# The experts' products of a decoder layer on one core: matmuls of 512 columns made as two of 256

## The chip, the cores and the metric
One core of a Trainium2 chip runs the whole kernel. The metric is the device time of one execution in microseconds (us), the median of several runs.

## The reference
A pre-norm decoder layer in fp32 on x of shape (8, 256, 512): attention, a convolution over a context, and a mixture of experts, each added to x. Only the last part is touched by the change:

```
probs = softmax(x @ Wr + br); top_vals, top_idx = top_k(probs, 3)      # 12 experts
for e in range(12):
    mask = (top_idx == e).any(-1)
    w_e  = sum of the gate weights of e / max(count of e, 1)
    h    = relu(x @ w1[e] + b1[e])          # 512 -> 1280
    h    = h @ w2[e] + b2[e]                # 1280 -> 512
    out += mask * (w_e * h)
out *= 1 - 0.8 * (sigmoid(relu(mean(out) @ Wp1 + bp1) @ Wp2 + bp2) > 0.7)
```

## The kernel before, in words
The kernel goes through three stages: attention (to about 220 us), the convolution with the router's logits and the routing (to about 540 us), and the experts, in `experts()` from line 1540. Only the last is changed.

Routing sorts the tokens by expert into 59 tiles (NTILE) of 128 rows, each of one expert. For every tile five engines work hand in hand; each runs its own program, written out by hand, and they meet at semaphores:

- POOL gathers the rows of a tile into `xg` and later scatters the result `y` into `acc` in memory.
- PE (TensorE) turns `xg` in four transposes (`x_t`, line 1949, out to `ps_xd`). ACT copies them out as `xf` and rounds them to `xh`; POOL subtracts to get the remainder `xl` (L1808).
- PE makes the **first product** (`first_product`, lines 1955 to 1971): 128 rows by 1280 columns of `h`, in three chunks (CHUNKS: 512, 512 and 256 columns), each in its own bank of `ps_h`. Since values are split into a high and a low part, a chunk is 4 x (xh by w_hi, L1964; xh by w_lo, L1965) and then 4 x (xl by w_hi, L1969): 12 matmuls. xh or xl is the weight that is loaded into the array, the expert's matrix is what streams, so the width of a matmul is the number of columns of the matrix. The matmul that ends a chunk raises `h_done`, and ACT copies the chunk out (L1886) and raises `h_evac`.
- PE turns `h` in ten transposes (`h_t`, L1977), ACT adds the bias and takes the relu (L1895), rounds all of it to `hh` (L1899), and POOL makes the remainder `hl` (L1812).
- PE makes the **second product** (`second_product`, lines 1981 to 1993): 20 matmuls with `hh` (L1987 with w_hi, L1988 with w_lo) and 10 with `hl` (L1991), all 512 columns wide into `ps_y`. The last raises `y_done`, ACT scales `y` out (L1905).

PE's order for tile i is: transposes of h of tile i, first product of tile i+1, transposes of x of tile i+2, second product of tile i. A loop (L2038) holds two tiles; 28 turns of it and three single tiles make the 59. Ahead of each product PE's sequencer reads the number of the expert into a register (`expert_of`, L1943: a TENSOR_LOAD and register operations), since the buffer of the weights (`e % 2`) depends on it. From it come the addresses: ahead of each matmul at L1964, L1965, L1987 and L1988 there is one register operation, ahead of those at L1969 and L1991 none.
DVE meanwhile splits the next expert's weights (L1687, L1689) that SP brings in, and frees a buffer by `h_done` and `y_done` of the first tile of an expert.

## Time and profile before

| | us |
|---|---|
| median of 3 runs | 1478.84 |
| lowest and highest | 1478.68, 1481.39 |
| the profiled execution, its own time | 1480.42 |
| its span, first to last instruction | 1478.6 |

In this span, by the profile's page, PE is busy 1360.2 us, PE's weight loads 1130.1 us (beside the matmuls), DVE 827.3, ACT 697.4, POOL 844.7; the mean granted clock of TensorE is 0.956 of full.

How to read it: PE is the matmuls, PEld the weight loads, PEq or PEldq what PE's sequencer does by itself (reads into registers, register operations, waits). The profile does not count the sequencer's work as busy. A matmul's duration runs over the start of the next one, since they are pipelined: the pace is read from start to start, not from the duration.

### The profile page before, as it was taken

How to read it: one execution, taken by the hardware profiler on the slowest of the kernel's cores; microseconds unless marked ns; L12 is line 12 of the kernel's file. 1: busy time of each engine (PE TensorE's matmuls, PEld its weight loads, DVE VectorE, ACT ScalarE, POOL GpSimd, SP SyncE). 2: the span in 40 equal slices, each digit the busy share in tenths (PEclk: the TensorE clock that was granted, in tenths of full speed). 3: DMA queues.
4: the chain of work that ended last, by engine and by line, in shares of the span. 5: the costliest groups of instructions: out<-in, count | busy, mean ns of one | idle time of the engine just before them, and what ended most of it. 6: DMA issues, size and time to landing. Idle time of an engine off the chain costs nothing.

```text
span 1478.6 us, 27777 instructions
## 1 busy us (share of the span) xinstructions
PE 1360.2 (92%) x7868; PEld 1130.1 (76%) x7869; DVE 827.3 (56%) x1197; ACT 697.4 (47%) x1878; POOL 844.7 (57%) x955
## 2 busy tenths in 40 slices
PE   5899998799996369999999999999999999999993
PEld 4677776577775258888888888888888888888883
DVE  6788887499997986647174435547443553000013
ACT  3656666154553424445444454544445444444530
POOL 0456545244564056767677677676766767565540
PEclk8999999799997679999999999999999999999996
DMA  7000000163333425545264435446443543251146
GB/s 271 1 1 0 0 0 27 47 214 100 105 112 114 185 77 159 125 116 157 47 169 102 121 87 133 107 109 170 106 126 81 139 106 78 37 162 35 29 133 237
DMA packets 77576, 152.42 MB, mean 103 GB/s; under 512 B 9120, under 2 KB 13728, under 8 KB 77024
## 3 DMA queue, kind: packets, MB, share of 16 engines
q1 hardware_dynamic: 62496, 115.09, 24.6%
q0 software_dynamic: 14320, 35.40, 12.1%
q10 hardware_dynamic: 720, 1.44, 0.3%
q8 instruction: 21, 0.34, 0.1%
q14 instruction: 19, 0.16, 0.0%
HBM read 119.31 MB, written 32.59 MB: 103 GB/s over the span
## 4 chain that ended last, share of the span: by engine, by line
PE 61%; DMA 2%; SPq 0%; DVE 0%; issue 0%; ACT 0%; DVEq 0%; POOL 0%; POOLq 0%
PE ps_h L1964 9%; PE ps_h L1965 9%; PE ps_h L1969 9%; PE ps_y L1987 9%; PE ps_y L1988 9%; PE ps_y L1991 9%; PE ps_td L1977 4%; PE ps_xd L1949 2%; DMA w_lo<-acc 1%; DMA w_hi<-acc 1%; DMA xg<-xnd,gi 0%; DMA acc<-y,si 0%; PE ps_xd L1998 0%; SPq L1673 0%; SPq L1668 0%
## 5 line engine op out<-in xcount | busy, mean ns | idle before, releaser
L1964 PE MATMUL ps_h<-w_hi,xh 128*128 x708 | 247.0, 361 | 1.5 <-ACT xh L1880 1.4
L1965 PE MATMUL ps_h<-w_lo,xh 128*128 x708 | 242.2, 354 | 0.0
L1987 PE MATMUL ps_y<-w_hi,hh 128*128 x590 | 236.9, 402 | 0.0
L1988 PE MATMUL ps_y<-w_lo,hh 128*128 x590 | 231.9, 393 | 0.0
L1689 DVE TENSOR_TENSOR w_lo<-stage,w_hi 128x512 f32 x220 | 214.4, 975 | 28.6 <-DVE w_hi L1687 2.9
L1822 POOL TENSOR_TENSOR y<-y,b_sb 128x512 f32<-128x512 f32 x58 | 80.1, 1382 | 210.2 <-ACT y L1905 210.2
L1812 POOL TENSOR_TENSOR hl<-h,hh 128x1280 fp32r<-128x1280 f32 x59 | 182.9, 3100 | 16.7 <-ACT hh L1899 16.2
L1886 ACT ACTIVATE h<-ps_h 128x512 f32<-128x512 f32 x177 | 80.6, 527 | 198.6 <-POOL hl L1812 190.9
L1905 ACT ACTIVATE y<-ps_y,wt 128x512 f32<-128x512 f32 x59 | 40.6, 688 | 275.4 <-PE ps_y L1991 275.4
L1969 PE MATMUL ps_h<-w_hi,xl 128*128 x708 | 164.1, 354 | 0.0
L1895 ACT ACTIVATE h<-ps_td,b_now 128x128 f32<-128x128 f32 x590 | 158.6, 391 | 3.9 <-PE ps_td L1977 1.2
L1964 PEld LDWEIGHTS ps_h<-w_hi,xh 128*128 128x128 f32 x708 | 133.6, 189 | 22.3 <-issue 2.2
L1965 PEld LDWEIGHTS ps_h<-w_lo,xh 128*128 128x128 f32 x708 | 133.6, 189 | 20.3
L1687 DVE CAST w_hi<-stage 128x512 f32 x220 | 143.8, 654 | 6.5 <-DMA stage<-in_wcat 6.0
L1991 PE MATMUL ps_y<-w_hi,hl 128*128 x590 | 144.9, 392 | 0.0
L1730 DVE TENSOR_TENSOR turn<-cst 128x1 f32<-128x1 f32 x11 | 3.7, 333 | 241.0 <-PE ps_h L1969 241.0
L1969 PEld LDWEIGHTS ps_h<-w_hi,xl 128*128 128x128 f32 x708 | 119.8, 188 | 19.0
L1991 PEld LDWEIGHTS ps_y<-w_hi,hl 128*128 128x128 f32 x590 | 110.8, 188 | 24.4
L1988 PEld LDWEIGHTS ps_y<-w_lo,hh 128*128 128x128 f32 x590 | 111.5, 189 | 22.5
L1987 PEld LDWEIGHTS ps_y<-w_hi,hh 128*128 128x128 f32 x590 | 111.5, 189 | 22.1
L1837 POOL DMA_INDIRECT acc<-y,si x59 | 101.4, 1719 | 27.2 <-issue 14.8
L1808 POOL TENSOR_TENSOR xl<-xf,xh 128x512 fp32r<-128x512 f32 x59 | 78.0, 1321 | 38.5 <-ACT xh L1880 37.8
(256 smaller groups left out, 2566.7 us busy)
## 6 DMA issues: line engine op xcount, KB each, us to landing
stage<-in_wcat SPq DMA_DIRECT2D x220, 256.0 KB
front<-in_ctx_rev SPq DMA_DIRECT2D x32, 192.0 KB, 2.4
w_lo<-in_wcat SPq DMA_DIRECT2D x4, 1280.0 KB, 12.2
acc<-added_c POOLq DMA_DIRECT2D x1, 4352.0 KB, 17.4
front<-kpad SPq DMA_DIRECT2D x16, 256.0 KB, 3.4
toe<-kpad SPq DMA_DIRECT2D x16, 256.0 KB, 3.4
x2d<-xs SPq DMA_DIRECT2D x16, 256.0 KB, 2.4
xnd<-xn_c SPq DMA_DIRECT2D x16, 256.0 KB, 2.0
```

What stands on the lines that cost most here:

```text
L1687: nc.vector.tensor_copy(hi, stage[:, c % NSTAGE]).then_inc(w_rounded, 1)
L1689: nc.vector.tensor_tensor(lo, stage[:, c % NSTAGE], hi.bitcast(F32), ALU.subtract).then_inc(split_done, 1)
L1812: nc.gpsimd.tensor_tensor(hl[:], h[:], hh[:].bitcast(F32), ALU.subtract).then_inc(hl_ready, 1)
L1837: pool.indirect_dma_start(acc, bass.IndirectOffsetOnAxis(ap=si[:, par:par + 1], axis=0), y[:, par], None, compute_op=ALU.add).then_inc(add ...
L1886: nc.scalar.activation(h[:, lo:hi], ps_h[:, c, 0:hi - lo], ACT.Copy).then_inc(h_evac, 1)
L1895: last = nc.scalar.activation(h[:, k * P:(k + 1) * P], ps_t[:, k // 4, (k % 4) * P:(k % 4 + 1) * P], ACT.Relu, bias=b1_now[:, k:k + 1])
L1964: nc.tensor.matmul(out, x_hi, part(w_hi, e, k * FF + lo, hi - lo), start=(k == 0), stop=False)
L1965: nc.tensor.matmul(out, x_hi, part(w_lo, e, k * FF + lo, hi - lo), start=False, stop=False)
L1969: last = nc.tensor.matmul(out, xl[:, k * P:(k + 1) * P], part(w_hi, e, k * FF + lo, hi - lo), start=False, stop=(k == KD - 1))
L1987: nc.tensor.matmul(ps_y[:], h_hi, part(w_hi, e, KD * FF + k * D, D), start=(k == 0), stop=False)
L1988: nc.tensor.matmul(ps_y[:], h_hi, part(w_lo, e, KD * FF + k * D, D), start=False, stop=False)
L1991: last = nc.tensor.matmul(ps_y[:], hl[:, k * P:(k + 1) * P], part(w_hi, e, KD * FF + k * D, D), start=False, stop=(k == KF - 1))
```

## The change
Both products are made in pieces of 256 columns (HALF_N). In the first product each chunk of 512 is done as two halves in sequence: all 12 matmuls of the left half, then all 12 of the right, into the two halves of the same bank; `h_done` is still raised once, behind the second half. The second product is done as two halves of 30 matmuls, `y_done` once behind the second. The wait for `xl_ready` and that for `hl_ready` stand in the first half alone, so they come after 8 and 20 matmuls of 256 columns.

```diff
--- before.py
+++ after.py
@@ -1576,6 +1576,7 @@
         ps_x = psum("ps_xd", [P, 512])
         ps_h = psum("ps_h", [P, 3, 512])
         ps_y = psum("ps_y", [P, 512])
+        HALF_N = 256
         CHUNKS = [(0, 512), (512, 1024), (1024, FF)]
         ps_pool, ps_late = ps_x[:, 0:KD * B], [ps_h[:, 1 + n, 0:KD * B] for n in range(LATE)]
         ps_hid, ps_z = ps_t[:, 0], ps_t[:, 1, 0:B]
@@ -1956,18 +1957,19 @@
                 pe.wait_ge(split_done, e * NCHUNK + N1)
                 pe.wait_ge(xh_ready, i + 2)
                 for c, (lo, hi) in enumerate(CHUNKS):
-                    out = ps_h[:, c, 0:hi - lo]
                     if not first:
                         pe.wait_ge(h_evac, 3 * i + c - 2)
-                    for k in range(KD):
-                        x_hi = xh[:, k * P:(k + 1) * P]
-                        nc.tensor.matmul(out, x_hi, part(w_hi, e, k * FF + lo, hi - lo), start=(k == 0), stop=False)
-                        nc.tensor.matmul(out, x_hi, part(w_lo, e, k * FF + lo, hi - lo), start=False, stop=False)
-                    if c == 0:
-                        pe.wait_ge(xl_ready, i + 2)
-                    for k in range(KD):
-                        last = nc.tensor.matmul(out, xl[:, k * P:(k + 1) * P], part(w_hi, e, k * FF + lo, hi - lo),
-                                                start=False, stop=(k == KD - 1))
+                    for at in range(lo, hi, HALF_N):
+                        out = ps_h[:, c, at - lo:at - lo + HALF_N]
+                        for k in range(KD):
+                            x_hi = xh[:, k * P:(k + 1) * P]
+                            nc.tensor.matmul(out, x_hi, part(w_hi, e, k * FF + at, HALF_N), start=(k == 0), stop=False)
+                            nc.tensor.matmul(out, x_hi, part(w_lo, e, k * FF + at, HALF_N), start=False, stop=False)
+                        if at == 0:
+                            pe.wait_ge(xl_ready, i + 2)
+                        for k in range(KD):
+                            last = nc.tensor.matmul(out, xl[:, k * P:(k + 1) * P], part(w_hi, e, k * FF + at, HALF_N),
+                                                    start=False, stop=(k == KD - 1))
                     last.then_inc(h_done, 1)
 
             def h_t(i):
@@ -1982,14 +1984,18 @@
                 pe.wait_ge(split_done, e * NCHUNK + NCHUNK)
                 pe.wait_ge(hh_ready, i + 1)
                 pe.wait_ge(y_evac, i + 1)
-                for k in range(KF):
-                    h_hi = hh[:, k * P:(k + 1) * P]
-                    nc.tensor.matmul(ps_y[:], h_hi, part(w_hi, e, KD * FF + k * D, D), start=(k == 0), stop=False)
-                    nc.tensor.matmul(ps_y[:], h_hi, part(w_lo, e, KD * FF + k * D, D), start=False, stop=False)
-                pe.wait_ge(hl_ready, i + 2)
-                for k in range(KF):
-                    last = nc.tensor.matmul(ps_y[:], hl[:, k * P:(k + 1) * P], part(w_hi, e, KD * FF + k * D, D),
-                                            start=False, stop=(k == KF - 1))
+                for at in range(0, D, HALF_N):
+                    out = ps_y[:, at:at + HALF_N]
+                    for k in range(KF):
+                        h_hi = hh[:, k * P:(k + 1) * P]
+                        nc.tensor.matmul(out, h_hi, part(w_hi, e, KD * FF + k * D + at, HALF_N), start=(k == 0), stop=False)
+                        nc.tensor.matmul(out, h_hi, part(w_lo, e, KD * FF + k * D + at, HALF_N), start=False, stop=False)
+                    if at == 0:
+                        pe.wait_ge(hl_ready, i + 2)
+                    for k in range(KF):
+                        last = nc.tensor.matmul(out, hl[:, k * P:(k + 1) * P],
+                                                part(w_hi, e, KD * FF + k * D + at, HALF_N),
+                                                start=False, stop=(k == KF - 1))
                 last.then_inc(y_done, 1)
 
             def pool_early(b):
```

On PE's queue, in the loop, at the end of the part with `xh` of the first chunk of the first product (`ps_h` is the chunk's bank, `w_hi` and `w_lo` the matrix; an ISA row is a register operation of two steps, a REGISTER_ALU row one of one step; the loads of the weights xh and xl aren't listed, there is one ahead of each matmul). Before:

```order
L1964 MATMUL ps_h<-w_hi,xh 128x512
L1965 REGISTER_ALU
L1965 MATMUL ps_h<-w_lo,xh 128x512
L1969 MATMUL ps_h<-w_hi,xl 128x512 [waits xl_ready]
L1969 MATMUL ps_h<-w_hi,xl 128x512 x3
L1961 REGISTER_ALU
L1964 ISA [waits h_evac]
L1964 MATMUL ps_h<-w_hi,xh 128x512
```

and with the change:

```order
L1966 MATMUL ps_h<-w_hi,xh 128x256
L1967 REGISTER_ALU
L1967 MATMUL ps_h<-w_lo,xh 128x256
L1971 MATMUL ps_h<-w_hi,xl 128x256 [waits xl_ready]
L1971 MATMUL ps_h<-w_hi,xl 128x256 x3
L1966 ISA
L1966 MATMUL ps_h<-w_hi,xh 128x256
L1967 REGISTER_ALU
```

Behind the four matmuls with xl there now stands the right half of the same chunk, with its own register operations and without a wait; before, the next chunk stood there.

The same engine at the end of the part with `hh` of the second product, before:

```order
L1987 MATMUL ps_y<-w_hi,hh 128x512
L1988 REGISTER_ALU
L1988 MATMUL ps_y<-w_lo,hh 128x512
L1989 REGISTER_ALU
L1991 MATMUL ps_y<-w_hi,hl 128x512 [waits hl_ready]
L1991 MATMUL ps_y<-w_hi,hl 128x512 x9
L1974 REGISTER_ALU
L1977 MATMUL ps_td<-cst,h 128x128 [waits relu_done,h_evac]
```

and with the change:

```order
L1991 MATMUL ps_y<-w_hi,hh 128x256
L1992 REGISTER_ALU
L1992 MATMUL ps_y<-w_lo,hh 128x256
L1994 REGISTER_ALU
L1996 MATMUL ps_y<-w_hi,hl 128x256 [waits hl_ready]
L1996 MATMUL ps_y<-w_hi,hl 128x256 x9
L1991 ISA
L1991 MATMUL ps_y<-w_hi,hh 128x256
```

The matmuls with hl, and the wait for it, come after the first 20 of 256 columns; the right half follows, and only then the transposes of the next tile. In a tile the matmuls go from 66 to 120 beside the 14 transposes, those with a register operation ahead from 44 to 80; the loop's body goes from 440 to 728 instructions of PE (matmuls, weight loads, register operations).

## Rows read from the trace of the kernel before
**Rows 1.** The page: busy time by engine, slices of PE, granted clock.
```profile
PE 1360.2 (92%) x7868; PEld 1130.1 (76%) x7869; DVE 827.3 (56%) x1197; ACT 697.4 (47%) x1878; POOL 844.7 (57%) x955
...
PE   5899998799996369999999999999999999999993
...
PEclk8999999799997679999999999999999999999996
```
**Rows 2.** Busy time in the stretch 560 to 1400 us, all engines.
```profile
core 0: us, PE busy (x) PEld busy (x) DVE busy (x) ACT busy (x) POOL busy (x), PEclk, DMA share, GB/s
560.00:1400.00 840.00, 840.00 (x4397) 713.69 (x4396) 346.04 (x453) 395.73 (x989) 574.84 (x659) 1.00 0.43 109
```
**Rows 3.** The waits from 560 to 1397 us, the four largest.
```profile
engine line waited for: us in total, times, longest us
ACT y L1905 <- PE ps_y L1991: 243.7, 54, 4.8
DVE turn L1730 <- PE ps_h L1969: 241.0, 10, 35.5
POOL y L1822 <- ACT y L1905: 195.0, 55, 4.1
ACT h L1886 <- POOL hl L1812: 181.5, 55, 3.8
```
**Rows 4.** The chain of waits from 890 to 960 us: start, us, what.
```profile
892.71 2.29 PE ps_y L1991 x10
895.00 1.09 PE ps_td L1977 x10
...
900.68 0.92 PE ps_h L1969 x4
902.51 0.46 PE ps_h L1969 x4
...
953.85 2.29 PE ps_y L1991 x10
```
**Rows 5.** Timeline of PE in three tiles: start, us from start to end, instruction.
```profile
901.44 0.28 PE L1964 MATMUL ps_h<-w_hi,xh 128*128 x1
...
902.35 0.62 PE L1969 MATMUL ps_h<-w_hi,xl 128*128 x4
902.80 0.60 PE L1949 MATMUL ps_xd<-cst,xg 128*128 128x128 f32 x4
903.16 0.48 PE L1987 MATMUL ps_y<-w_hi,hh 128*128 x1
903.48 0.40 PE L1988 MATMUL ps_y<-w_lo,hh 128*128 x1
...
907.83 2.46 PE L1991 MATMUL ps_y<-w_hi,hl 128*128 x10
910.12 1.25 PE L1977 MATMUL ps_td<-cst,h 128*128 128x128 f32 x10
...
932.01 0.28 PE L1964 MATMUL ps_h<-w_hi,xh 128*128 x1
...
932.92 0.62 PE L1969 MATMUL ps_h<-w_hi,xl 128*128 x4
933.38 0.60 PE L1949 MATMUL ps_xd<-cst,xg 128*128 128x128 f32 x4
...
953.69 2.46 PE L1991 MATMUL ps_y<-w_hi,hl 128*128 x10
```
**Rows 6.** PE's queue, L1987 and L1988, 947 to 950.3: ns, first and last start.
```profile
L1987 PEldq FUSED_REGOPS  x10: 46/46/118, 947.8 to 950.1; - x10
L1988 PEldq ALU_OP  x10: 32/32/32, 948.0 to 950.2; - x10
```
**Rows 7.** PE's queue by line: L1965, L1961 near 910; L1982, L1984 near 947.
```profile
L1965 PEldq ALU_OP  x4: 32/32/32, 909.5 to 910.3; - x4
L1961 PEldq ALU_OP  x1: 32/32/32, 910.6 to 910.6; - x1
L1982 PEldq FUSED_REGOPS  x1: 47/47/47, 947.6 to 947.6; - x1
L1984 PEldq EVENT_SEMAPHORE  x1: 51/51/51, 947.7 to 947.7; - x1
```
**Rows 8.** PE's queue at the first read of the expert, L1943 and L1964.
```profile
L1943 PEldq FUSED_REGOPS  x2: 42/96/151, 954.2 to 954.6; - x2
L1943 PEldq TENSOR_LOAD <-eid x1: 306/306/306, 954.3 to 954.3; - x1
L1964 PEldq FUSED_REGOPS  x6: 46/46/104, 955.2 to 956.8; - x6
```
**Rows 9.** PE's queue at the second read, L1943, in four tiles; L1987 after one.
```profile
L1943 PEldq FUSED_REGOPS  x2: 42/96/151, 946.9 to 947.3; - x2
L1943 PEldq TENSOR_LOAD <-eid x1: 299/299/299, 947.0 to 947.0; - x1
L1943 PEldq TENSOR_LOAD <-eid x1: 1002/1002/1002, 763.5 to 763.5; - x1
L1943 PEldq TENSOR_LOAD <-eid x1: 1019/1019/1019, 1222.1 to 1222.1; - x1
L1943 PEldq FUSED_REGOPS  x2: 42/96/151, 824.6 to 825.8; - x2
L1943 PEldq TENSOR_LOAD <-eid x1: 1056/1056/1056, 824.7 to 824.7; - x1
L1987 PEldq FUSED_REGOPS  x1: 118/118/118, 826.3 to 826.3; - x1
```
**Rows 10.** Timeline of ACT and POOL and of PE near 947; hl in all tiles.
```profile
945.06 1.27 ACT L1899 ACTIVATE hh<-h 128x1280 fp32r<-128x1280 f32 x1
946.42 3.21 POOL L1812 TENSOR_TENSOR hl<-h,hh 128x1280 fp32r<-128x1280 f32 x1
949.02 0.48 PE L1987 MATMUL ps_y<-w_hi,hh 128*128 x1
L1812 POOL TENSOR_TENSOR hl<-h,hh x55: 2945/3014/3539, 564.0 to 1389.4; 128x1280 fp32r<-128x1280 f32 x55
```
**Rows 11.** DMA queue that loads code, 600 to 1390 us: packets, MB, share of 16 engines.
```profile
q14 instruction: 1, 0.01, 0.0%
```

## The prediction
> **What bounds the kernel now.** I read the page's busy line and slices first [rows 1]: TensorE (PE) is busy 92% of the span and from the sixteenth slice on nearly without a gap, at the full granted clock. That stretch is the experts' loop. Then the busy time of one stretch of it [rows 2]: from 560 to 1400 us PE is busy 840.00 of 840.00 us at a clock of 1.00, its weight loads (PEld) 713.69 us. In the waits of the same stretch [rows 3] everybody waits for PE or for POOL, and no row has PE as the one that waits. So here a nanosecond of PE's pace is a nanosecond of the kernel, and all else counts only if it comes to stop PE. The chain of waits [rows 4] gives the period: from one run of ten L1991 to that four tiles later 953.85 - 892.71 = 61.14 us, 15.285 us for a tile, 59 tiles.
>
> **Term 1: the pace of the matmuls.** Per tile the change turns 24 matmuls of 512 columns in the first product and 30 in the second into 108 of 256; 12 of 256 and 14 transposes stay. The columns streamed are the same; the weight loads of these go from 54 to 108. What a matmul of 256 costs when it stands in a row of its like is to be seen already, in the third chunk. In start times [rows 5]: the ten L1991 take 910.12 - 907.83 = 2.29 us, and the 19 matmuls ahead of them 907.83 - 903.48 = 4.35 us, so 0.2289 us at 512 columns. The twelve of the third chunk take 902.80 - 901.44 = 1.36 us, in another tile 933.38 - 932.01 = 1.37 us, and their first eight 0.91 us in both. That is 0.1136 us each with the turn to the transposes in it, and between 0.905/8 = 0.1131 and 0.915/8 = 0.1144 without. The weight loads do not stop it: the transposes, one load for each 128 columns, go at 1.09/10 = 0.109 us [rows 4], below 0.1133. I take 0.1134: two halves are 0.2268 us against 0.2289, 2.1 ns less. 54 x 59 = 3186 pairs x 2.1 ns = 6.7 us gained. The ends: 2.7 ns, 8.6 us gained, and 0.1 ns, 0.3 us gained.
>
> The Trainium skill ("TensorE: Matmul & The Clock Gate", section "Back-to-back issue gap") has a matmul cost its columns at 2.4 GHz and about 2.5 ns on top, so that two of 256 would cost 2.5 ns more than one of 512; by it this term would be 3186 x 2.5 ns = 8.0 us lost. The rows at 0.1133 and 0.2289 do not show such a fixed part; they show a price a little under proportion.
>
> **Term 2: whether PE's sequencer can feed it.** This is new. Each matmul and each weight load has to be issued, and ahead of each matmul with xh or hh stands one register instruction that works out an address. In the rows of PE's queue [rows 6] the ten L1987 register operations go from 947.8 to 950.1 and the ten L1988 ones from 948.0 to 950.2: 2.2/9 = 0.244 us for two matmuls, 0.122 each. That is slower than the array at 256 columns (0.1134), where at 512 it had twice the time. A matmul without one (L1969, L1991) costs the sequencer far less. Bounds: from the last L1965 at 910.3 to L1961 at 910.6 [rows 7] it issues one matmul that belongs to the register operation and four more, 0.3 - 0.1 = 0.2 us, 0.05 each, though the queue was full there, so this is a ceiling. And register operations with nothing between them (L1982 at 947.6, L1987 at 947.8, one between) stand 0.1 apart, with a matmul between them 0.122: 0.02 each is the floor. I take 0.03, nearer the floor because the ceiling has waiting in it.
>
> A piece of 12 (8 with a register operation, 4 without) then costs the sequencer 8 x 0.122 + 4 x 0.03 = 1.10 us and the array 12 x 0.1134 = 1.36. A half of the second product: 20 x 0.122 + 10 x 0.03 = 2.74 against 3.40. So on average it keeps up. The trouble can only be where it stands still: it reads the expert's number twice a tile (L1943). How far it is ahead there: the first read begins at 954.2 [rows 8], when the array has started three of the ten L1991 that began at 953.69; the other seven and the ten transposes are queued, **17 matmuls**. Before the change that is 7 x 0.229 + 10 x 0.109 = 2.7 us of cover, after it 7 x 0.1134 + 1.09 = 1.88. Its next register operation of the product is at 955.2, so with the first issue some 1.2 us go by: 0.7 us of lead is left. Five pieces of 12 win 0.26 us each, three waits cost 0.1 each: +1.0, so the queue is nearly full again at the second read. There the cover is 13 x 0.1134 + 0.44 = 1.91 us; a read of 0.30 us costs 1.05 us (946.9 to 947.8 and the issue), one of 1.056 us, the longest [rows 9], 1.8 us (824.6 to 826.3 and the issue). Then the 20 matmuls with register operations lose 20 x 0.009 = 0.17 us more. So only reads over some 0.8 us run the array dry, for about 0.2 us each. There are six of them over 0.9 us in the 59 tiles (three stand in the rows); with one a little shorter that is 7 x 0.2 = **1.4 us lost**. The two ends: nothing, and the first rival.
>
> **Terms at nothing.** The second product's first half reaches the hl matmuls after 20 x 0.1134 = 2.27 us instead of 4.58, and hl comes from POOL. In the tile shown [rows 10] POOL ends hl at 946.42 + 3.21 = 949.63; the second product starts at 949.02, so hl is asked for at 951.3 and is 1.7 us early. The longest hl takes 3.54 us instead, 0.3 us later; 1.3 us stay. With that cover gone PE would wait for each hl by the shortfall. hh, which the sequencer waits for at L1984, ends at 945.06 + 1.27 = 946.33, 1.4 us before it gets there (947.7). xl for a tile is made in the tile before. h_done and y_done still come once a chunk and once a tile, so ACT, DVE and SP see the same events. The loop's code grows from 440 to 728 PE instructions; from 600 to 1390 us the trace has a single load of code [rows 11], so the loop of 440 stayed in place, and no row shows a loop of 728.
>
> **Sum.** -6.7 + 1.4 = -5.3 us. The profiled execution took 1480.4 us for a span of 1478.6, 1.6 us over the median of 1478.84 of the three runs. Against its own time that is 1475.1; against the median, **1473.5 us**. What a measurement of this kernel can tell from no change is about 0.2%, 3 us: 1475.9 to 1481.8.
>
> **Rivals.**
> First, the slower side: **the sequencer becomes the bound.** If a matmul without register operation costs it 0.05 us (the ceiling) and not 0.03, its work for a tile is 80 x 0.122 + 54 x 0.05 + 1.2 for the first read, 1.3 for the second with its longer ones and 0.5 for waits and the loop's branch = 15.5 us, against the array's 15.285 - 0.11 = 15.17. Then the lead is never won back and each tile takes some 15.4 to 15.5: 59 x (15.45 - 15.285) = +9.7, about 1488 us. It decides at about 0.045 us a matmul, or with 0.03 at about 0.13 us for one with a register operation. For it: 0.122 is already over 0.1134, and the margin is 5% of a tile. Against it: the ceiling was read where the queue was full.
> The Trainium skill ("TensorE: Matmul & The Clock Gate", section "Architectural detail: the array is 16× 32×32, not 1× 128×128") gives TensorE a queue of 64 instructions; that would be 32 matmuls with their loads, where [rows 5, 8] show 17, and with it term 2 would be nothing and the time 1472.1.
>
> Second: **two halves cost what the whole did.** The chain [rows 4] has the four L1969 of 256 at 0.46 us and of 512 at 0.92: no gain. Then term 2 alone is left: 1478.84 + 1.4 = 1480.2. If that 0.46/4 = 0.115 is the pace of long stretches and 0.2289 stays that of the wide ones, a fixed part of each matmul shows, two halves lose 1.1 ns, and 3.5 us more give 1483.7. The fixed part that the Trainium skill states (page and section as under term 1) would be larger than this. For it: three stretches of 12 are all that a trace of before shows, and rounded. Against it: 0.91 us for eight, twice.
>
> Third: **hl late.** It would need hl 1.3 us later than its longest; then 1 us a tile would be 59 us, a time of 1532. POOL's work does not change, so I give it next to nothing.
>
> **How the numbers follow.** The forecast has 0.64 (1470.2 to 1475.9, from 8.6 gained and nothing lost to a gain of 3); the second rival 0.19, most of it within 0.2%; the first 0.15 and the third 0.02. Faster 0.64; same 0.18; slower 0.18. The range leaves out the first rival's upper half and the third: 1470.2 to 1485.
>
> **What would show it.** In the profile of after: PE busy all of 560 to 1390 us or with idle time of a few us in all, on L1991's successor (the first matmuls with hh) right after the second read; a tile of 15.17 to 15.2 us; twelve matmuls in 1.36 us in every chunk, thirty in 3.40 in each half of the second product; no wait of PE for hl or hh. Wrong would be: twelve in more than 1.38 us (the second rival), pitches of 0.122 us through whole stretches with register operations (the first), a wait of PE for hl L1812, or loads of code in every turn of the loop.

## The result and the profile after

| | us |
|---|---|
| changed kernel, median of 4 runs | 1502.46 (1501.01 to 1503.20) |
| kernel before, median of 4 runs on the same chip | 1478.76 (1475.79 to 1481.39) |
| ratio, 95% interval | 1.016 (1.0139 to 1.0181) |
| profiled execution, its own time and span | 1501.01, 1499.2 |

The change costs 23.7 us; the forecast was 5 us gained. Five more runs of it in a later comparison gave 1499.51 to 1501.58. The ratios and intervals given below count only runs within 1.5% of the fastest run of the same kernel.

The page of the changed kernel, busy time, to hold against [rows 1]:

```profile
PE 1382.3 (92%) x11054; PEld 1288.8 (86%) x11055; DVE 823.3 (55%) x1197; ACT 697.3 (47%) x1878; POOL 834.2 (56%) x955
```

PE is busy 22.1 us longer, and the span is longer by nearly the same (20.6); POOL is busy 10 us less, DVE and ACT 4 us or less away from before. The same stretch as in [rows 2]:

```profile
560.00:1400.00 840.00, 840.00 (x7184) 840.00 (x7183) 337.64 (x448) 384.95 (x960) 551.57 (x644) 1.00 0.44 107
```

PE is again busy all of 840.00 us at a granted clock of 1.00, so no gap and no slower clock took the time. What is new is that the weight loads fill the stretch as well, 840.00 us against 713.69. The waits of 560 to 1397 us, as in [rows 3], have the same partners as before; the two longest, shown here, have grown by some 15 us each. Still none is PE's:

```profile
ACT y L1906 <- PE ps_y L1996: 260.3, 53, 5.2
DVE turn L1731 <- PE ps_h L1971: 255.7, 10, 37.9
```

So PE works without a break, and each step takes longer. The chain of waits (start, us, what), against [rows 4]:

```profile
899.19 1.18 PE ps_y L1996 x10
900.37 1.09 PE ps_td L1979 x10
...
902.41 0.47 PE ps_h L1971 x4
...
908.54 0.44 PE ps_xd L1950 x4
...
930.54 1.18 PE ps_y L1996 x10
```

From 899.19 to 930.54 are two tiles: 15.675 us each against 15.285 before. 0.39 x 59 = 23.0 us, the whole loss within 1 us. Ten matmuls of 256 columns take 1.18 us; the transposes are unchanged at 1.09 and 0.44. The timeline of PE (start, us from start to end, instruction) over three pieces of twelve and the third chunk:

```profile
902.72 0.28 PE L1966 MATMUL ps_h<-w_hi,xh 128*128 x1
...
906.96 0.28 PE L1966 MATMUL ps_h<-w_hi,xh 128*128 x1
...
908.37 0.60 PE L1950 MATMUL ps_xd<-cst,xg 128*128 128x128 f32 x4
```

Three pieces from 902.72 to 906.96 are 36 matmuls in 4.24 us: **0.1177 us each**, not 0.1134. The last piece, 906.96 to 908.37, is the third chunk, whose instructions the change did not touch: 1.41 us for twelve, where [rows 5] have 1.36 and 1.37. Whatever it is, it sits in the pace of every 256-wide matmul, old or new.

The sum closes with it. Two halves cost 0.2354 us for 0.2289: 6.5 ns x 3186 pairs = 20.7 us. The third chunk: 12 x 4.4 ns x 59 = 3.1 us. Together 23.8 us, measured 23.7.

Does the sequencer cause it? Its register operations are the L1991 and L1992 rows, the read is L1944 (queue rows near 908 of the changed kernel: count, ns min/median/max, first and last start):

```profile
L1944 PEldq TENSOR_LOAD <-eid x1: 939/939/939, 906.7 to 906.7; - x1
L1991 PEldq FUSED_REGOPS  x20: 46/46/113, 908.2 to 913.0; - x20
L1991 PE MATMUL ps_y<-w_hi,hh x13: 279/279/365, 908.7 to 912.8; 128*128 x13
```

Even behind a read of 939 ns the first register operation stands half a microsecond ahead of its matmul. And the four matmuls with xl, which have no register operation, go at 0.47/4 = 0.1177 like the rest. Matching every register operation with its matmul between 600 and 1390 us gives the same for the whole stretch: they stand 3 to 18 matmuls ahead of the one that the array has started. So the array goes slower while its queue has work for it.

The trace of before had shown the same in its first two tiles, and the prediction did not look at them. The chain of the kernel before from 541 to 567 us:

```profile
541.75 0.47 PE ps_h L1969 x4
...
550.89 0.47 PE ps_h L1969 x4
...
566.20 0.46 PE ps_h L1969 x4
```

In its timeline the twelve of the third chunk go from 549.79 to 551.20 (1.41 us) in one tile and from 565.13 to 566.50 (1.37 us) in the next. So a 256-wide matmul with its load has **two paces here: 0.1133 and 0.1177 us**. Of the 59 third chunks in the trace of before the first two are slow and the other 57 quick; the changed kernel runs at the slow pace. The experiments ask what holds it there.

### The profile page after: what moved, and what is told of

It is laid out like the page before. It is cut to its first block, busy times and chain, and to the rows that moved or that the text cites. A ratio compares the mean times of both kernels' runs of the same rounds, so it can differ in the third digit from the quotient of the medians.

```text
span 1499.2 us, 36273 instructions
## 1 busy us (share of the span) xinstructions
PE 1382.3 (92%) x11054; PEld 1288.8 (86%) x11055; DVE 823.3 (55%) x1197; ACT 697.3 (47%) x1878; POOL 834.2 (56%) x955
## 3 DMA queue, kind: packets, MB, share of 16 engines
q0 software_dynamic: 14320, 35.40, 12.3%
## 4 chain that ended last, share of the span: by engine, by line
PE 61%; DMA 2%; POOL 0%; SPq 0%; issue 0%; ACT 0%; DVE 0%; DVEq 0%; POOLq 0%
PE ps_h L1971 9%; PE ps_h L1966 9%; PE ps_h L1967 9%; PE ps_y L1996 9%; PE ps_y L1991 9%; PE ps_y L1992 9%; PE ps_td L1979 4%; PE ps_xd L1950 2%; DMA w_hi<-acc 1%; DMA w_lo<-acc 1%; DMA xg<-xnd,gi 0%; DMA acc<-y,si 0%; SPq L1674 0%; POOL hl L1813 0%; POOL acc L1838 0%
## 5 line engine op out<-in xcount | busy, mean ns | idle before, releaser
L1966 PE MATMUL ps_h<-w_hi,xh 128*128 x1180 | 296.6, 284 | 1.5 <-ACT xh L1881 1.4
L1967 PE MATMUL ps_h<-w_lo,xh 128*128 x1180 | 291.5, 280 | 0.0
L1991 PE MATMUL ps_y<-w_hi,hh 128*128 x1180 | 289.5, 284 | 0.0
L1992 PE MATMUL ps_y<-w_lo,hh 128*128 x1180 | 284.5, 280 | 0.0
L1966 PEld LDWEIGHTS ps_h<-w_hi,xh 128*128 128x128 f32 x1180 | 222.0, 188 | 2.1 <-issue 2.1
L1992 PEld LDWEIGHTS ps_y<-w_lo,hh 128*128 128x128 f32 x1180 | 222.7, 189 | 0.0
L1991 PEld LDWEIGHTS ps_y<-w_hi,hh 128*128 128x128 f32 x1180 | 222.7, 189 | 0.0
L1967 PEld LDWEIGHTS ps_h<-w_lo,xh 128*128 128x128 f32 x1180 | 222.4, 188 | 0.0
L1971 PEld LDWEIGHTS ps_h<-w_hi,xl 128*128 128x128 f32 x1180 | 160.0, 188 | 0.3 <-POOL xl L1809 0.3
L1996 PEld LDWEIGHTS ps_y<-w_hi,hl 128*128 128x128 f32 x1180 | 147.1, 188 | 0.3 <-POOL hl L1813 0.3
```

What stands on the lines that cost most here:

```text
L1966: nc.tensor.matmul(out, x_hi, part(w_hi, e, k * FF + at, HALF_N), start=(k == 0), stop=False)
L1967: nc.tensor.matmul(out, x_hi, part(w_lo, e, k * FF + at, HALF_N), start=False, stop=False)
L1971: last = nc.tensor.matmul(out, xl[:, k * P:(k + 1) * P], part(w_hi, e, k * FF + at, HALF_N), start=False, stop=(k == KD - 1))
L1991: nc.tensor.matmul(out, h_hi, part(w_hi, e, KD * FF + k * D + at, HALF_N), start=(k == 0), stop=False)
L1992: nc.tensor.matmul(out, h_hi, part(w_lo, e, KD * FF + k * D + at, HALF_N), start=False, stop=False)
L1996: last = nc.tensor.matmul(out, hl[:, k * P:(k + 1) * P], part(w_hi, e, KD * FF + k * D + at, HALF_N), start=False, stop=(k == KF - 1))
```

## The experiments

In what follows "quick" is 0.1133 us and "slow" 0.1177 us for a matmul of 256. By the sizes above a kernel's time is worked out as: each pair of halves -2.1 ns quick or +6.5 ns slow, x 59, and 3.1 us more if the third chunk is slow. Diffs are against the changed kernel unless said otherwise; 59 is the number of tiles. Experiments 1, 2, 3, 7, 8, 9 and 12 are a single execution each.

**1. Who stands ahead: the narrow chunk first.** The kernel before, with only the order of widths changed, so that the chunk of 256 comes right behind the ten transposes of h.

```diff
-        CHUNKS = [(0, 512), (512, 1024), (1024, FF)]
+        CHUNKS = [(0, 256), (256, 768), (768, FF)]
```

> The kernel before, with the chunk of 256 columns first and the two of 512 behind it, so that the same twelve matmuls of 256 now come right behind the ten transposes of h instead of behind a matmul of 512. Theory A (a run of 256 keeps the pace that it gets at its start: 0.1133 us behind a 512, 0.1177 behind a transpose): twelve in about 1.41 us instead of 1.36, the tile 0.05 us longer, about 1482 us in all. Theory B (0.1177 comes from the weight loads having no rest anywhere in the tile): 0.1133 us as before, twelve in 1.36, 1478.8 us. Theory C (the sequencer's issue): 0.1133 as before, since twelve matmuls are covered by its lead, 1478.8 us.

One run: 1482.52 us, the nine runs of before beside it 1476.44 to 1481.24 (median 1478.98). In its chain:

```profile
895.51 1.09 PE ps_td L1977 x10
897.54 0.47 PE ps_h L1969 x4
899.85 0.91 PE ps_h L1969 x4
```

The narrow chunk is slow in every tile, the chunks of 512 unchanged: 3.1 us expected from the pace, 3.5 measured. The chain shows it; the time alone would not, since the runs of before spread over 4.8 us. The same twelve matmuls, moved from behind 512-wide ones to behind transposes, are slow. Neither their number nor the register operations changed.

**2. Only the second chunk in halves.** Second product and first chunk stay whole (`wide = HALF_N if c == 1 else hi - lo`).

> Only the second chunk of the first product is made in halves: 36 matmuls of 256 in a row behind twelve of 512; the rest as before. Theory A: all 36 at 0.1133 us, 4.08 us in all, the tile 0.027 us shorter, about 1477 us. Theory B: the pace is between the two or falls from 0.1133 to 0.1177 within the run, up to 4.24 us for the 36 and 1486 us. Theory C: the matmuls behind a register operation drift towards 0.122 us once the lead is used, those with xl stay at 0.1133.

One run: 1478.24 us, where 12 pairs x 2.1 ns x 59 = 1.5 us less than before were to be had, below what one run can tell. 36 matmuls of 256 stand in a row behind twelve of 512, quick in all tiles but the first. Its chain:

```profile
897.37 0.45 PE ps_h L1972 x4
```

**3. Only the second product in halves.** The first product as before.

> Only the second product is made in halves; the first as before. Theory A: the 60 behind the transposes of x go at 0.1177 us, 7.06 us instead of 6.87; the chunk of 256 in the first product stays at 0.1133 (1.36 us for twelve); about +0.19 us a tile, 1490 us. Theory B: the 60 between 0.1133 and 0.1177, and the chunk of 256 slower too. Theory C: as A in the part with hh, but the matmuls with hl at 0.1133.

One run: 1474.81 us, quick in all tiles but the first and the end of the last, though the 60 stand right behind the four transposes of x. Theory A as it stood, that any transposes ahead make the pace slow, is false. Its chain:

```profile
902.61 1.13 PE ps_y L1995 x10
...
917.81 1.14 PE ps_y L1995 x10
```

**4. A 512-wide matmul at the head of each product** of the changed kernel:

```diff
+                nc.tensor.matmul(ps_y[:], hh[:, 0:P], part(w_hi, e, KD * FF, D), start=True, stop=False)
                 for at in range(0, D, HALF_N):
...
+                        if k:
+                            nc.tensor.matmul(out, h_hi, part(w_hi, e, KD * FF + k * D + at, HALF_N), start=False, stop=False)
```

> The changed kernel, but the first matmul of each product (k = 0 with the high part of the matrix) is 512 wide over both halves, so that every run of 256 begins behind a 512. Theory A: all 256-wide matmuls at 0.1133 us, a tile of about 15.17 us, 1472 us: faster than both. Theory B and C: no change against the changed kernel, 0.1177 us, a tile of 15.67 us, 1502 us.

Five runs, 1503.87 us (1501.21 to 1505.05), ratio 1.0166 (1.0151 to 1.018). Slow everywhere. One wide matmul at the entry does not do it.

**5. The first tiles wide.** The first four tiles stand outside the loop with matmuls of 512; only the last second product ahead of the loop, and everything in it, is in halves. It asks whether the start decides.

```diff
-            with pe.Fori(0, PAIRS) as j:
+            for j in range(WIDE_PAIRS):
+                tile(2 * j, j, 0, True, True, True)
+                tile(2 * j + 1, j, 1, True, True, True)
+            with pe.Fori(WIDE_PAIRS, PAIRS) as j:
```

> The changed kernel, but the first four tiles of the experts' stage are taken out of the loop and made as before the change (first products of 512, 512 and 256 columns, second products of 512, the last of them in halves); the loop of the other 26 pairs is all in halves. Theory D (a 256-wide run has two paces, 0.1133 and 0.1177 us; the state is carried through transposes and kept by 256-wide runs, and only stretches of 512 switch it): the second product before the loop is at 0.1133 and so is every tile of the loop, 15.17 us a tile, about 1472 us. Theory E (the quick pace needs a stretch of 512 in every tile): 0.1177 us from the first product of the loop on, 15.67 us a tile, about 1501 us.

Four runs, 1500.05 us (1499.45 to 1501.51), ratio 1.0136 (1.0117 to 1.0154). Its chain shows the quick pace being lost:

```profile
601.94 1.14 PE ps_y L1999 x10
603.08 1.09 PE ps_td L1981 x10
605.11 0.47 PE ps_h L1973 x4
```

The second half of the second product is quick (1.14), the ten transposes follow, and from the next matmul of 256 on the loop is slow to its end. A quick start is not enough.

**6. First chunk wide**, the rest in halves (`wide = hi - lo if c == 0 else HALF_N`), so that twelve matmuls of 512 stand between the transposes of h and the first of 256.

> The changed kernel, but the first chunk of the first product is 512 wide: behind the ten transposes of h stand twelve matmuls of 512, and all the rest of the tile is 256 wide. Theories D and E both allow the quick pace: 96 and 12 matmuls of 256 at 0.1133 us, a tile of 15.19 us, 1473 us, if twelve of 512 are enough; if they are not, 0.1177 us and about 1498 us.

Four runs, 1497.33 us (1496.26 to 1499.63), ratio 1.0123 (1.0102 to 1.0144). Quick at first, until this second product, in its timeline:

```profile
627.07 0.28 PE L1992 MATMUL ps_y<-w_hi,hh 128*128 x1
...
628.20 0.28 PE L1992 MATMUL ps_y<-w_hi,hh 128*128 x1
...
628.65 0.28 PE L1992 MATMUL ps_y<-w_hi,hh 128*128 x1
...
629.01 0.28 PE L1993 MATMUL ps_y<-w_lo,hh 128*128 x1
```

Ten steps from 627.07 to 628.20 are 0.113 each; from 628.65 on they are 0.12, and stay at 0.1177 for the rest of the loop. Just ahead of this the sequencer had read the expert's number, and its register operations (queue rows, L1944 and, from 628.5 to 629.0 us, L1993):

```profile
L1944 PEldq TENSOR_LOAD <-eid x1: 1034/1034/1034, 624.8 to 624.8; - x1
L1993 PE MATMUL ps_y<-w_lo,hh x3: 276/278/280, 628.3 to 628.8; 128*128 x3
L1993 PEldq ALU_OP  x2: 32/32/32, 628.6 to 628.8; - x2
```

Here the register operations (628.6, 628.8) have the matmuls of the same line (at 628.77 and 629.01 in the timeline) only some 0.2 us behind them, with the weight load in between: the array, at 0.113 a matmul, had used up its queue behind a read of 1.03 us and met the sequencer at its 0.122. The place coincides; that it is the cause, this run alone does not show. Until then five tiles in a row had been quick, with all but the first chunk in halves.

**7. Second chunk wide**, the first in halves right behind the ten transposes.

> As the run before, but the second chunk is the wide one and the first is in halves: the 24 behind the transposes of h are 256 wide, then twelve of 512, then 256 for the rest. If what counts is what stands behind the transposes of h (as when the narrow chunk was put first), the 24 go at 0.1177 us and those behind the wide chunk may go at either: 0.1133 us if twelve of 512 switch the state, a tile of 15.30 us and 1480 us; 0.1177 us if not, 1499 us.

One run: 1498.5 us, slow throughout. 42 pairs x 6.5 ns x 59 + 3.1 = 19.2 us over the 1478.8 of before give 1498.0.

**8. One transpose of h more** (the first is made twice, eleven in a row), to shift the phase by 0.109 us.

> The changed kernel with the first of the ten transposes of h made twice (0.109 us more a tile, 6.4 us in all). If the pace hangs on the instant at which the run of 256 begins behind the transposes, one more may switch it: 0.1133 us and 1478 us. If it does not hang on that (theory E, and D in its plain form), 0.1177 us stays and the time is 1509 us.

One run: 1507.94 us; slow in the whole loop, and 0.109 x 59 = 6.4 us for the transpose. An odd number did no better than an even one. The second product of the last tile, behind the 48 small matmuls of the pooling, begins at the half clock. When the clock is back it is quick, in a kernel whose products have no matmul of 512 (a window with its granted clock of 0.50, and the chain):

```profile
1466.40:1469.40 3.00, 3.00 (x15) 3.00 (x15) 0.00 (x0) 0.00 (x0) 3.00 (x3) 0.50 0.61 87
...
1470.20 1.13 PE ps_y L1996 x10
```

**9. Twelve transposes of h** in the kernel of experiment 5.

> The kernel with the wide prologue (e6), in which the pace of 0.1133 us held through the four transposes of x and was lost behind the ten of h, with two of the ten transposes of h made twice, so twelve (0.218 us more a tile, 12.9 us in all). If what decides is the instant at which the run of 256 begins, and four transposes keep the pace, so do three times four: 0.1133 us in the loop until the array catches up with the sequencer somewhere, 1485 us if it never does. If ten or more transposes always lose it: 0.1177 us from the first product of the loop on, 1513 us.

One run: 1514.49 us. The second product ahead of the loop was slow already, so this run can't say what the number does. Its trace shows two things beside that. Four third chunks ahead of the loop, all behind 24 matmuls of 512, alternate: slow, quick, slow, quick (0.47, 0.46, 0.47 and 0.46 us for the four with xl at 549.44, 564.96, 580.50 and 596.02). And the slow second product comes straight behind the last, quick one: the pace was lost across the four transposes of x.

**10. The read moved.** Experiment 6, with the expert's number for the second product read behind the first chunk, where the queue holds 512-wide matmuls.

```diff
                     last.then_inc(h_done, 1)
+                    if then is not None and c == 0:
+                        read = then()
```

> The kernel with the first chunk wide and all else in halves (e7), but the read of the expert's number for the second product is issued right behind the first chunk of the first product instead of ahead of the second product, where the sequencer has most lead. Theory F (the state of 256-wide runs falls from 0.1133 to 0.1177 us when the array catches up with the sequencer, as it did in e7 at 628.7 us behind a long read, and then stays there though the queue is full again): the array never catches up, 0.1133 us in all tiles, a tile of 15.19 us, about 1473 us, faster than before. Theory G (the fall in e7 had nothing to do with the sequencer): as e7, some 1497 us, with a fall early in the stage.

Fourteen runs in two heaps: six from 1470.17 to 1475.87 us and eight from 1496.26 to 1501.28, nothing between. The sizes give 42 pairs x 2.1 ns x 59 = 5.2 us gained in the quick case, 1472.7 against the 1477.86 of before in this comparison, and 19.2 lost in the slow one, 1497.1. The middles of the heaps are 1472.8 and 1497.9. The ratio, 0.9964 (0.9949 to 0.998), is that of the first heap alone; as a kernel it is a coin toss. The profiled run was one of the upper heap, and its first product in the loop was still quick; the second product behind it, four transposes of x later, was slow, and all of the loop from there on:

```profile
547.04 0.46 PE ps_h L1972 x4
...
550.29 1.18 PE ps_y L2000 x10
```

The register operations of that second product begin at 546.31 us for a matmul at 547.89, 15 matmuls ahead, so here the pace was lost with a well filled queue. That moving the read brought the lower heap isn't shown either: with eight of fourteen in the upper one, experiment 6 would have all of its four there by chance in one case of nine.

**11. The second product alone, timed.** The kernel of experiment 3 once more.

> The kernel of e2 once more, timed in rounds: only the second product in halves. 0.1133 us for its 60 matmuls in all tiles but the first, 30 x 2.1 to 2.3 ns = 0.063 to 0.069 us a tile less than before, 3.7 to 4.1 us in all: about 1475 us, ratio 0.997.

Twelve runs: nine from 1471.45 to 1477.28 us (middle 1473.46) and three of 1491.22, 1493.09 and 1493.67. The ratio 0.9989 (0.9964 to 1.0015) counts eleven of them, those of 1491.22 and 1493.09 us too; the middle of the nine is 0.997 of before's 1477.86. Worked out: 1474.1 quick, 1492.5 slow. The profiled run was one of the three, and its chain stands beside that of experiment 3, for **the same code**:

```profile
894.12 1.18 PE ps_y L1995 x10
...
902.84 0.47 PE ps_h L1970 x4
...
909.65 1.18 PE ps_y L1995 x10
```

A tile takes 909.65 - 894.12 = 15.53 us here and 15.20 us in experiment 3. From 600 to 1400 us the two traces agree in what else is seen: a granted clock of 1.00, weight loads busy 748 and 747 of 800 us, a DMA share of 0.43 in both. So the pace isn't a property of the instructions; it is a state that an execution gets into and keeps. Here too it was lost across the four transposes of x, in the first second product of the loop, and the 24 matmuls of 512 in every tile behind it did not bring it back once.

**12. The second read made twice**, in the kernel of experiment 3, to let the array catch up with the sequencer in every tile.

> The kernel with only the second product in halves (e2, 0.1133 us in all tiles), with the read ahead of the second product made twice, some 0.5 us more in which the sequencer issues nothing. Theory F: the array catches up in the second product, which falls to 0.1177 us or more in many tiles, up to 0.26 us a tile beside the delay itself; 1485 to 1495 us; the 24 matmuls of 512 may bring the pace back each time. Theory G: only the delay, at most 0.1 to 0.2 us where reads are long, the pace stays 0.1133; about 1478 us.

One run: 1498.82 us. Its chain from 560 to 600 us:

```profile
564.44 0.46 PE ps_h L1970 x4
...
567.95 1.18 PE ps_y L1995 x10
...
580.22 0.47 PE ps_h L1970 x4
...
595.73 0.46 PE ps_h L1970 x4
```

The third chunk, behind 24 matmuls of 512, finds the quick pace in two of these three tiles, and the second products behind the doubled read are slow by their end here. From 547 us on nine of 58 third chunks are quick, the last at 1141 us. So a stretch of 512 can bring the quick pace back but need not.

The doubled read lets the array catch up: the register operations then stand two matmuls ahead and now and then a matmul starts late. In such a place the pace changes, and in both directions. At 598.2 and at 865.0 us a quick second product turns slow. At 1098 us a slow one turns quick (timeline, then chain):

```profile
1097.09 0.28 PE L1991 MATMUL ps_y<-w_lo,hh 128*128 x1
...
1097.68 0.33 PE L1990 MATMUL ps_y<-w_hi,hh 128*128 x1
...
1099.34 1.13 PE ps_y L1995 x10
```

Five steps to 1097.68 take 0.59 us, 0.118 each; then come matmuls that start late, and the ten with hl take 1.13 us. It stayed quick until the queue ran low again in the next tile. No matmul of 512 stands in between. The time is some 6 us over what experiment 11 took at the slow pace; the second read may have cost them, and they were not taken apart.

**13. The first product alone in halves**, right behind the ten transposes; the second product whole.

> Only the first product in pieces of 256; the second stays in matmuls of 512. The pieces of 256 stand right behind the ten transposes of h. Theory A (256-wide matmuls keep one of two paces, 0.1133 or 0.1177 us, for as long as they follow each other; behind the ten transposes of h they always take the slow one): all 60 at 0.1177 in every tile, 24 pairs x 6.5 ns + 12 x 4.4 ns = 0.209 us a tile, x 59 = 12 us more, about 1490 us, in every one of the timed runs. Theory B (the pace of the expert stage is drawn once per execution, and the place does not matter): some runs near 1475 us with 0.1133 everywhere, some near 1490.

Six runs, 1491.32 us (1488.91 to 1492.92), before 1478.02, ratio 1.0091 (1.0075 to 1.0107). Slow in every run, by its time, as Theory A has it: 12.3 us worked out, 13.3 measured. In its chain the narrow matmuls are slow and the ten of 512 with hl take what they took before:

```profile
895.74 2.29 PE ps_y L1993 x10
...
900.07 0.47 PE ps_h L1971 x4
```

It also splits the change: about 12 us of its loss come with the first product, which includes the third chunk's 3.1, and 30 pairs x 6.5 ns x 59 = 11.5 us with the second.

**14. Ten transposes of x.** Experiment 3's kernel with six more transposes of x: each of the four a second time and two a third.

```diff
-                for k in range(KD):
+                for k in (*range(KD), *range(KD), KD - 2, KD - 1):
                     last = nc.tensor.transpose(ps_x[:, k * P:(k + 1) * P], xg[:, par, k * P:(k + 1) * P], ident)
```

> The kernel with the second product alone in halves, and x turned with ten transposes for four (six are made twice): is it the number of transposes ahead of the 256-wide matmuls that loses the fast pace? The six more cost 6 x 0.109 us x 59 = 38.6 us. Theory A (number of transposes ahead decides): always slow behind them, 30 pairs x 6.5 ns + 12 x 4.4 ns = 0.248 us a tile, 14.6 us more than the fast runs of the same kernel without the six, so 1473 + 38.6 + 14.6 = about 1526 us every time. Theory B (it is something else than their number, such as what stands ahead of the transposes: here 512-wide and 256-wide matmuls of the first product): mostly 1512 us, some runs at 1526, as without them.

Six runs, 1530.19 us (1527.92 to 1537.13). All slow by their times, where with four transposes nine of twelve were quick. In the chain, 1.09 for the ten, then 1.18:

```profile
891.46 1.09 PE ps_xd L1950 x10
894.91 1.18 PE ps_y L1995 x10
```

It agrees with Theory A, number and all (1526 expected). But the third chunk behind the 512-wide ones is slow too (907.15, 0.47 for four), as in the trace of experiment 11, so here both places share the pace; in those of experiments 9 and 12 they did not always.

**15. The changed kernel again.**

> The changed kernel once more, timed more often. Theory A (both products behind or fed by the slow stretch behind the transposes of h): every run between 1500 and 1505 us. Theory B (drawn per execution, as with the second product alone in halves, where a quarter of the runs were slow): some runs near 1476 us (1478.8 less the 6.7 us of the forecast's first term, and with the code and reads as they are).

Five runs, 1500.27 us (1499.51 to 1501.58), before 1478.02, ratio 1.0154 (1.0138 to 1.0171). By their times none of the nine runs was quick. Yet the profiled one was, for a while. Its chain, the four matmuls with xl of three pieces of twelve; the ten transposes of h stand between the first and the second:

```profile
537.57 0.47 PE ps_h L1971 x4
...
541.16 0.59 PE ps_h L1971 x4
...
542.65 0.45 PE ps_h L1971 x4
```

Behind the transposes the matmuls were slow at first (540.41 to 540.88 in the timeline, four in 0.47 us). The sequencer was then only two matmuls ahead, two matmuls started 0.02 and 0.10 us late, and from 541.25 on the pace was quick, within a row of matmuls of 256. It held through the rest of the first product, the four transposes of x and the second product:

```profile
553.30 1.14 PE ps_y L1996 x10
556.47 0.47 PE ps_h L1971 x4
```

The same step as in experiment 5: quick ahead of the ten transposes, slow behind them, and slow for the rest of the loop.

**16. No long row of transposes.** If that row is the cause, breaking it up must help. The transposes of h of the next tile go in pairs between the last ten matmuls with hl:

```diff
+                        if at and then_t and k % 2:
...
+                            h_part((k - 1, k))
```

> The changed kernel, with the ten transposes of h of the next tile no longer in a row: two of them behind every second one of the last ten matmuls with hl, the last two behind the last. So never more than four 128-wide transposes follow each other. Theory A (a long row of transposes right ahead of the 256-wide matmuls loses the fast pace of 0.1133 us): fast in many or all of the runs, 1478 - 6.7 = 1471 us, and 4 more turns from transposes to matmuls a tile at some 8 ns (28 + 201 against 113 + 109 ns) give 2 us back: about 1473. Theory B (256-wide matmuls of this kernel run at 0.1177 whatever stands between them): every run at 1501 to 1505 us.

Five runs, 1503.55 us (1502.88 to 1505.71), ratio 1.0181 (1.0165 to 1.0196). Slow in every run, by its time; a piece in its timeline:

```profile
920.76 0.63 PE L1971 MATMUL ps_h<-w_hi,xl 128*128 x4
922.17 0.63 PE L1971 MATMUL ps_h<-w_hi,xl 128*128 x4
```

1.41 us from one piece of twelve to the next. Theory A falls: in a loop of 256-wide matmuls alone a long row of transposes is not needed to stay at the slow pace. (This trace had it from the stage's first tiles on, so it does not show what a pair of transposes does to a quick pace.)

**17. Its control:** the kernel before with the same placing in pairs.

> The control: the kernel before, all chunks and the second product as there (512 wide), with the same placing of the transposes in pairs between the last ten matmuls with hl. Theory A: the pace of the 512-wide matmuls is the same with either history (0.2289 us), so placing alone brings nothing: 1476 to 1481 us. Theory B: the same. Should the placing itself be worth something (relu and hh of the next tile start no earlier), it shows here.

Twelve runs, 1480.68 us (1478.61 to 1486.54), before 1476.88, ratio 1.0022 (1.001 to 1.0035). At the upper edge of what was expected: the placing itself costs 3.8 us by the medians. That is far too little to hide a quick pace in experiment 16, which is some 30 us over what that would give (1480.7 less 6.7).

## What the runs say together

Shown: the two paces; that the whole loss is their difference; that the same code runs at either (3 and 11, and the two heaps of 10). The 256-wide matmuls right behind the transposes of h started slow in the loop of every trace that has such (1, 4, 5, 7, 8, 9, 13, 15, 16), and the times of the other runs of these kernels fit the slow pace. All kernels that were quick over nearly a whole run have at least twelve matmuls of 512 between the transposes of h and the first of 256.

Where the pace changes, the traces show these kinds of place:

- Across a row of transposes it was lost, with 8 to 15 matmuls in the queue: two traces across the ten of h (5, 15), three across the four of x (9, 10, 11). Across the four of x it also held, in nearly every tile of experiment 3.
- Where the array had caught up with the sequencer, two matmuls ahead, it was lost (6, 12) and found (12, 15).
- In the last tile, behind matmuls at the half clock, it was found (8, 9, 11) and lost (3).
- Behind a stretch of 512 it was found in 12 and in the kernel before (between 550.89 and 566.20), and not once in 57 tiles of the trace of 11.

So the changed kernel can find the quick pace without a matmul of 512, and did in 15. Its loop then lost it at the next ten transposes of h.

Left open: what in the array differs between the paces; what decides, in each such place, which of the two comes out; why the ten transposes of h were followed by the slow one each time where the four of x mostly kept the quick one. A row of ten isn't necessary (16), and four are not always harmless (9, 10 and 11). An emptied queue isn't necessary either (5, 10, 11, 15). Where a kernel ran once, its pace is that of one execution.

No kernel here is surely better than the one before. The best, the second product alone in halves, is 0.3% faster by the middle of its nine quick runs and 1% slower in a quarter of its runs.

## Why the prediction was wrong, point by point

- **What bounds the kernel**: right. PE is busy 840.00 of 840.00 us before and after, and each nanosecond of its pace came out in the time. One row was misread on the way: not everybody in [rows 3] waits for PE or POOL, POOL's y waits for ACT (195.0 us). It changes nothing, since ACT's y waits for PE.
- **Term 1, the pace**: this is the step that failed. "What a matmul of 256 costs when it stands in a row of its like is to be seen already, in the third chunk", and it was taken at 0.1134: three stretches of twelve, all from tiles in the quick state, were taken as the price of a matmul of 256. The changed kernel has 0.1177: +20.7 us where the term had -6.7, and +3.1 for the third chunk, which the prediction held to be untouched. As the price of the quick state the term was right: the nine quick runs of experiment 11 are 4.4 us under before at their middle (3.7 worked out), the six of experiment 10 5.1 us (5.2 worked out). The sign was lost by reading a state as a constant, and the rows that tell otherwise, the third chunk at 541.75 and 550.89, were in the trace. It held 59 such stretches; "three stretches of 12 are all that a trace of before shows" is wrong.
- **The transposes as a witness** ("The weight loads do not stop it", since the transposes, one load for each 128 columns, go at 0.109): this didn't carry over. The transposes keep 0.109 at either pace; they tell nothing about matmuls of 256.
- **Term 2, the sequencer**: +1.4 us forecast, nothing seen. Behind a read of 0.94 us it was still 0.5 us ahead. Partly that is because a slower array asks less of it; at the quick pace experiment 6 shows it caught up, as the term had it, and there the pace changed with it. The lead of 17 matmuls was read rightly: with register operations and matmuls matched in this way from 600 to 1390 us (in all traces but that of experiment 4) the sequencer was never more than 18 matmuls ahead, so the rival with 32 in the queue has nothing for it here.
- **The terms at nothing**: hl, hh, xl and the code were right. No row of the waits has PE waiting, and from 600 to 1390 us the queue that loads code has a single packet, as in [rows 11].
- **The rivals**: the second one ("two halves cost what the whole did", with a fixed part of each matmul showing) had the right sign. Its fixed part, from 0.115 against 0.2289, was 1.1 ns a pair and gave at most 1483.7 us, where 6.5 ns were measured; and a fixed part has no room for the quick pace, at which a pair gains 2.1 ns. Its own sign was met: twelve matmuls in over 1.38 us, 1.41. The rule of the Trainium skill cited in term 1 ("TensorE: Matmul & The Clock Gate", "Back-to-back issue gap") had the right sign: 2.5 ns a pair, 8.0 us lost. The section gives that rule for an isolated matmul, with no time for a weight load in it, which the prediction did not say. The trace agrees with it in sign only: the rule has one pace, and the measured price is 2.6 times its own. The first rival didn't come: no stretch goes at 0.122 throughout.
- **The range** took a pace between 0.1131 and 0.115 for its bounds. The slow pace lay in the trace and outside them.

## What to carry to other kernels

Before a pace is carried over to new instructions, read it in every place where the trace has it, the first tiles too: two values of one pattern, 3.9% apart, are a state, and the price of the change is a range between them. In this kernel, where the array is the bound, matmuls of 512 with a load each were safe (0.2289 us with either state) and matmuls of 256 a gamble of -2.1 or +6.5 ns for each pair, lost in every run in which they stood right behind the transposes of h in the loop. And a kernel whose runs fall in two heaps must be timed often: experiment 3's one run took 1474.81 us, the first one of the same code in experiment 11 took 1491.22.

## What was not expected of the hardware

- A 256-wide matmul with its weight load goes at 0.1133 or 0.1177 us at the same granted clock of 1.00, with matmuls waiting in the queue, and holds either for over 800 us (slow from 560 to 1400 us in the changed kernel, quick from 560 to 1419 us in experiment 3, in its third chunks and second products). At 512 columns no such difference is seen: ten take 2.29 us in the kernel before and in experiment 13, whose narrow ones are slow. The transposes (128 columns) keep 1.09 us for ten.
- The pace can differ between two executions of one program: 9 to 3 in experiment 11, 6 to 8 in experiment 10.
- It changes from one matmul to the next, in both directions: lost across four or ten transposes with matmuls waiting in the queue, lost or found where the array had caught up with the sequencer, found or lost behind the half clock (the last tiles of experiments 8 and 3).
- In this kernel the sequencer's register operations were never more than 18 matmuls, each with its load, ahead of the array.
